# The routing's keys behind the low part of the last outputs in a fused attention and expert kernel

## Chip, cores and metric

One core of one Trainium2 chip. The metric is the device time of one launch in microseconds (us), as the median of the runs.

## What is computed

A gated cross-attention layer and a mixture-of-experts layer on 32 batches of 256 tokens of width 256:

```
x = x + tanh(g_xattn) * LN_affine(softmax(q k^T / 8) v Wout)   # q from LN(x), 16 heads of 64,
                                                               # k, v from 77 context rows and one null row
h = LN(x)
w = top-8 of sigmoid(h Wr + br), divided by their sum          # 32 experts
x = x + tanh(g_ffn) * (shared(h) + sum_e w[t, e] * expert_e(h))
expert_e(h) = (silu(h Wg + bg) * (h Wu + bu)) Wd + bd          # width 128
```

Products in f32 are made as three products of a high part (rounded to fp32r) and a low part (the difference): `split_product` (L142). ScalarE makes the high part while it copies a bank out of PSUM, VectorE the low part by a subtraction.

## The kernel before

**Phases.** A context phase makes all keys and values and stores them in DRAM. Then the attention loop runs over steps b = -2 .. 33, and the expert phase over 16 dense rounds (the shared expert on all tokens) and 159 pages of 512 token rows, each page of one expert.

**A step of the attention loop.** Step b does the attention of batch b, the output projection, layer norms and x1 of batch b - 1, and the routing of batch b - 2. Each engine has a written order of work; semaphores alone tie the engines together.

- *TensorE* (`tensor`, `step` at L1401): `similarity(0)` and `similarity(1)`, the scores of half the heads for each of the two token tiles, and then the names of `RING` (L93) in order, each of which writes one of four PSUM banks: X (transpose of the next but one batch's normed x), N2 (transpose of the rows to be routed), Oa and Ob (output projection of the batch before, line L144 to L146 with `wo`), T0a .. T3b (transposes of probabilities), L (router logits), R (mask sums that give each row its place), Q0 .. Q3 (queries of the next batch), PV0a .. PV1b (outputs, transposed). Behind Oa stand `similarity(2)` and `similarity(3)`. `similarity(u)` waits until the exponentials of u - 2 are done, since it overwrites their scores (L1295). Oa waits until PV1b's low part of the step before is made (L1370). `free` (L1308) makes each name wait until its bank was evicted: T3a for PV0a's low part, R for `centre`, which reads Ob.
- *ScalarE* (`scalar`): the exponentials `exp` (L935), 32 a step, each with its sum, then the high parts (L947).
- *VectorE* (`vector`, `step` at L1218): `maximum(u)` (L1037) of scores, `normalise(u)` (L1043 to L1052), the low parts in the order of `EVICTED` (`low`, L1184), and between these, where `ROUTE_AFTER` (L109) says so, the stages of the routing (`route`, L1088). Layer norm: `statistics` (L1058, L1062), `centre` (z, L1070), `residual` (x1, L1078). The next batch's `maximum(0)` stands behind PV1a.
- *GpSimd* (`gpsimd`, `step` at L863): 16 indirect scatters a step (L854), which put the 256 rows of a batch eight times into pages; `weigh` (L861); x1's bias (L885); and `make_rstd` (L841 to L848), `make_rstd(1)` for the output norm, on which `centre` waits, and `make_rstd(2)` for the norm of x1.
- *SyncE* issues all plain DMAs.

**The routing's last stages.** `key` (L1142 to L1147) makes three results: key = (slot + 1) * mask, a new page_end, and top_key, the eight largest keys of a token. `kept` (L1151) turns top_key into kept_index, the row numbers that the scatters of the next step use. `match` (L1191) and `sum_weights` (L1201) read key and top_key in the next step. Line numbers are the same in both kernels.

`ROUTE_AFTER` names, for a low part, the stages that VectorE does right behind it. The keys were done behind PV1a, so after `maximum(0)` of the next batch and before PV1b's low part:

Of the kernel before, what the change touches and what calls it, by code (L numbers as in the profile page):

```python
# [106 lines left out]
AHEAD_FILLS, AHEAD_PAGES = 3, 3  # L107

ROUTE_AFTER = {"T1a": ["logits", "top", "mask"], "PV0b": ["placed"], "Q3": ["opened", "page", "moved", "slot"],  # L109
               "PV1a": ["key"], "PV1b": ["kept"]}  # L110

ROUTE = ["biased", "logits", "top", "without_top", "mask", "placed", "opened", "over", "page", "moved", "owner", "page_shift",
         "over_shift", "cursor", "grown", "slot", "key", "page_end", "top_key", "kept"]
# [1961 lines left out]
```

How the kernel before makes its waits and increments, by code:

```python
            def load_x(batch):  # L262
                if batch >= 3:
                    sp.wait_ge(tile_measured, batch - 1)
                sp.dma_start(x_rows[x_slot(batch)][:, :, 0:D], x_tiles[batch]).then_inc(tile_loaded[x_slot(batch)], 16)
# [1 line left out]
            def load_piece(i):  # L267
                if i >= STAGES:
                    sp.wait_ge(w_lo, i - STAGES + 1)
                sp.dma_start(staged(i), pieces[i][0]).then_inc(w_loaded[i % STAGES], 16)
# [19 lines left out]
            def step(g):  # L290
                for name in CRING:
                    if not made_in(name, g):
                        continue
                    if name[0] == "K" and int(name[2]) % KPART == KPART - 1:
                        i, unit = int(name[1]), key_unit(name, g)
                        first = int(name[2]) // KPART * KPART * M
                        sp.wait_ge(hi, at(CRING, name, g))
                        sp.dma_start(keys_out[:, g * CG + i * CBATCHES:g * CG + (i + 1) * CBATCHES, first:first + KPART * M],
                                     keys[unit % KSLOTS][:, :, :, :].rearrange("p b q m -> p b (q m)")).then_inc(keys_stored[unit % KSLOTS], 16)
                    if name[0:2] == "K1":
# [3 lines left out]
                    elif name[0] == "V" and name[2] == "1":  # L304
                        unit = value_unit(name, g)
                        sp.wait_ge(lo, at(CRING, name, g))
                        t = int(name[1])
# [108 lines left out]
            def moments(batch):  # L416
                dve.wait_ge(tile_measured, batch + 1)
                for t in range(TT):
```

## Time and profile before

| | us |
|---|---|
| median of 3 runs | 2119.76 |
| lowest, highest | 2118.06, 2122.13 |
| profiled execution | 2123.7 |
| its span in the profile | 2122.0 |
| TensorE busy | 1996.5 |
| VectorE busy | 1667.2 |
| ScalarE busy | 1384.1 |
| GpSimd busy | 1205.9 |

The granted TensorE clock is 0.977 on the mean. The profile is of one execution; DVE is VectorE, ACT ScalarE, POOL GpSimd, PE TensorE's matmuls and PEld its weight loads. An idle time in brackets stands before the instruction of its row, with what ended it. Times in a timeline are from the start of the span.

### The profile page before, as it was taken

The numbers are of one execution on the slowest core, as the hardware profiler recorded it, in microseconds if no ns is written. First come the engines' busy times: TensorE is split into PE (matmuls) and PEld (weight loads), VectorE is DVE, ScalarE is ACT, GpSimd is POOL, SyncE is SP. The second block draws the span as 40 slices with busy tenths as digits, with TensorE's granted clock in tenths as the row PEclk, the third lists the DMA queues.
The fourth block names the chain that finished last, engine by engine and source line by source line (L and its number), as shares of the span: only waits on it lengthen the run. The fifth ranks groups of instructions, "written<-read, shape, count | busy, mean of one in ns | idle before, by whom it ended". The sixth has DMA issues, their size and how long they took to land. (4 is left out here: it accounts for less than half of the span.)

```text
span 2122.0 us, 42583 instructions
## 1 busy us (share of the span) xinstructions
PE 1996.5 (94%) x13762; PEld 1832.7 (86%) x13762; DVE 1667.2 (79%) x3996; ACT 1384.1 (65%) x4030; POOL 1205.9 (57%) x1323
## 2 busy tenths in 40 slices
PE   7999689999999999999997899999999999999995
PEld 7888589999999999999986788989888888888884
DVE  4433158888888888888886766768999999999996
ACT  3322267777777777777773267777877777777771
POOL 0000203777777777777777500017777777777775
PEclk9999899999999999999997899999999999999997
DMA  9664678977777777777786999999999999999998
GB/s 279 211 192 169 243 219 268 293 241 242 241 243 245 244 246 244 246 244 235 246 266 221 330 336 287 286 293 385 404 401 398 396 393 389 395 395 393 392 362 281
DMA packets 401109, 625.61 MB, mean 295 GB/s; under 512 B 171000, under 2 KB 275161, under 8 KB 398425
## 3 DMA queue, kind: packets, MB, share of 16 engines
q1 hardware_dynamic: 351736, 488.60, 68.1%
q0 software_dynamic: 49152, 134.28, 17.6%
q8 instruction: 112, 1.84, 0.4%
q14 instruction: 109, 0.88, 0.1%
HBM read 315.08 MB, written 307.63 MB: 293 GB/s over the span
## 5 line engine op out<-in xcount | busy, mean ns | idle before, releaser
L1714 POOL DMA_INDIRECT parts<-results_dram,kept_index x512 | 517.7, 1011 | 382.6 <-DMA results_dram<-y 218.8
L854 POOL DMA_INDIRECT pages_dram<-rows,kept_index x512 | 509.9, 996 | 158.5 <-issue 139.2
L935 ACT ACTIVATE exps<-sim,minus_max 128x78 f32<-128x78 f32 x1024 | 321.0, 366 | 35.9 <-DVE minus_max L1037 35.7
L935 ACT ACTIVATION_READ_ACCUMULATOR exps<-sim,minus_max 128x1 f32 x1024 | 253.1, 248 | 0.0
L1735 ACT ACTIVATE w_h<-w_raw 128x768 fp32r<-128x768 f32 x159 | 134.0, 843 | 155.7 <-DMA w_raw<-in_experts 155.7
L1823 DVE SCALAR_TENSOR_TENSOR parts<-parts,kept_weight 128x256 f32<-128x256 f32 x448 | 213.6, 477 | 2.6 <-DMA parts<-dense_dram 1.4
L1920 PE MATMUL xps<-ident,xin 128*128 128x128 f32 x1272 | 167.2, 275 | 20.1 <-DVE wq_l L1785 9.8
L1797 DVE TENSOR_TENSOR w_l<-w_raw,w_h 128x768 fp32r<-128x768 f32 x159 | 151.7, 954 | 40.3 <-ACT w_h L1735 40.1
L144 PE MATMUL yps<-w_h,hid_h 128*128 128x256 f32 x636 | 179.5, 282 | 0.3
L146 PE MATMUL yps<-w_l,hid_h 128*128 128x256 f32 x636 | 178.8, 281 | 0.0
L145 PE MATMUL yps<-w_h,hid_l 128*128 128x256 f32 x636 | 178.5, 281 | 0.0
L1742 ACT ACTIVATE y<-yps 128x512 f32<-128x512 f32 x318 | 171.7, 597 | 1.5 <-PE yps L146 1.5
L1920 PEld LDWEIGHTS xps<-ident,xin 128*128 128x128 f32 x1272 | 140.8, 141 | 29.0 <-issue 24.1
L1299 PE MATMUL sim<-kT,qT 128*128 128x156 f32 x1024 | 155.5, 303 | 7.2 <-issue 3.8
L144 PE MATMUL ring<-xnT_h,wq_h 128*128 128x256 f32 x512 | 156.4, 305 | 3.7 <-DVE outT_l L1184 1.8
L1785 DVE TENSOR_TENSOR wq_l<-xps,wq_h 128x512 fp32r<-128x512 f32 x212 | 143.0, 686 | 18.5 <-ACT wq_h L1729 18.5
L1766 ACT ACTIVATE hid_h<-up_ps 128x512 fp32r<-128x512 f32 x175 | 103.3, 591 | 81.3 <-DVE up_ps L1874 80.1
L1299 PEld LDWEIGHTS sim<-kT,qT 128*128 128x128 f32 x1024 | 142.8, 194 | 12.4 <-issue 10.5
L144 PE MATMUL ring<-wo_h,outT_h 128*128 128x256 f32 x512 | 148.7, 290 | 3.4 <-DVE outT_l L1184 0.5
L1874 DVE SCALAR_TENSOR_TENSOR up_ps<-up_ps,w_raw,act_gate 128x512 f32<-128x512 f32 x159 | 120.1, 755 | 37.7 <-PE up_ps L146 36.2
L146 PE MATMUL ring<-xnT_l,wq_h 128*128 128x256 f32 x512 | 144.7, 283 | 0.0
L1037 DVE TENSOR_REDUCE minus_max<-sim 128x8 f32<-128x624 f32 x128 | 102.2, 799 | 54.0 <-PE sim L1299 54.0
(261 smaller groups left out, 6638.7 us busy)
## 6 DMA issues: line engine op xcount, KB each, us to landing
xin<-pages_dram SPq DMA_DIRECT2D x159, 512.0 KB, 10.7
results_dram<-y SPq DMA_DIRECT2D x159, 512.0 KB, 9.7
w_raw<-in_experts SPq DMA_DIRECT2D x159, 385.0 KB
pages_dram<-blank SPq DMA_DIRECT2D x108, 512.0 KB, 3.9
pages_dram<-blank SPq DMA_DIRECT2D x20, 1024.0 KB, 6.2
values_dram<-values SPq DMA_DIRECT2D x16, 1024.0 KB
v_main<-values_dram SPq DMA_DIRECT2D x64, 256.0 KB
keys_dram<-keys SPq DMA_DIRECT2D x16, 616.0 KB, 4.3
```

Of the source, the lines that this page charges most:

```text
L144: eng.matmul(out, left[0], right[0], start=start, stop=False)
L145: eng.matmul(out, left[1], right[0], start=False, stop=False)
L146: return eng.matmul(out, left[0], right[1], start=False, stop=stop)
L854: pool.indirect_dma_start(dram["pages"], bass.IndirectOffsetOnAxis(ap=kept_index[:, at:at + 1].bitcast(U32), axis=0), buffer(batch)[:, k / ...
L935: last = act.activation(exps[u % 2][:, h, :], scores(u)[:, h // 4, h % 4, :], ACT.Exp, bias=minus_max[u][:, h:h + 1], accum_out=row_sum[u] ...
L1299: last = pe.matmul(sim[u % 2][:, i // 2, (i % 2) * 2 * J:(i % 2 + 1) * 2 * J], qT[:, pair, tt * P:(tt + 1) * P], kT[:, pair, :], start=Tru ...
L1714: pool.indirect_dma_start(parts[slot(batch, t)][:, k, :], None, done, bass.IndirectOffsetOnAxis(ap=kept_index[:, at:at + 1].bitcast(U32), ...
L1742: last = act.activation(y[s][:, q:q + 2, :], yps[:, q:q + 2, :], ACT.Copy)
L1785: dve.tensor_tensor(xT[m % XT][1][:, c, :], xps[:, c, :], xT[m % XT][0][:, c, :].bitcast(F32), ALU.subtract).then_inc(x_lo, 1)
L1797: dve.tensor_tensor(w_split[s][1][:, :], w_raw[s][:, 0:EW], w_split[s][0][:, :].bitcast(F32), ALU.subtract).then_inc(w_lo, 1)
L1823: dve.scalar_tensor_tensor(out=out, in0=part[:, k, :], scalar=kept.weight[:, at:at + 1], in1=part[:, TOPK, :], op0=ALU.mult, op1=ALU.add). ...
L1920: last = pe.transpose(xps[:, c, q * P:(q + 1) * P], xin[s][:, q, c * P:(c + 1) * P], ident[:, :])
```

## The change

The stage `key` moves from behind PV1a to behind PV1b, in front of `kept`. Everything that the stages compute is as before.

```diff
-               "PV1a": ["key"], "PV1b": ["kept"]}
+               "PV1b": ["key", "kept"]}
```

Only VectorE's order differs. The first place is the end of a step in the middle of the loop (steps 2 to 30): outT_l is the low part of PV1a and then of PV1b, minus_max<-sim the next batch's first maximum and then its second. Before:

```order
L1139 TENSOR_TENSOR slot<-placed_to,over_shift 128x64
L1184 TENSOR_TENSOR outT_l<-ring,outT_h 128x512
L1037 TENSOR_REDUCE minus_max<-sim 128x8
L1142 SCALAR_TENSOR_TENSOR key<-slot,mask 128x64
L1144 TENSOR_TENSOR page_end<-page_end,grown 128x32
L1147 MAX top_key<-key 128x8 x2
L1184 TENSOR_TENSOR outT_l<-ring,outT_h 128x512
L1151 TENSOR_SCALAR kept_index<-top_key 128x16
L1037 TENSOR_REDUCE minus_max<-sim 128x8
```

And changed:

```order
L1139 TENSOR_TENSOR slot<-placed_to,over_shift 128x64
L1184 TENSOR_TENSOR outT_l<-ring,outT_h 128x512
L1037 TENSOR_REDUCE minus_max<-sim 128x8
L1184 TENSOR_TENSOR outT_l<-ring,outT_h 128x512
L1142 SCALAR_TENSOR_TENSOR key<-slot,mask 128x64
L1144 TENSOR_TENSOR page_end<-page_end,grown 128x32
L1147 MAX top_key<-key 128x8 x2
L1151 TENSOR_SCALAR kept_index<-top_key 128x16
L1037 TENSOR_REDUCE minus_max<-sim 128x8
```

PV1b's low part has moved up over four instructions (top_key is two), and kept_index now follows top_key directly.

The second place is step 31, the last with outputs, on VectorE again; there is no next batch, so no maximum stands there, and kept_weight is the first instruction of step 32. Changed:

```order
L1139 TENSOR_TENSOR slot<-placed_to,over_shift 128x64
L1184 TENSOR_TENSOR outT_l<-ring,outT_h 128x512 x2
L1142 SCALAR_TENSOR_TENSOR key<-slot,mask 128x64
L1144 TENSOR_TENSOR page_end<-page_end,grown 128x32
L1147 MAX top_key<-key 128x8 x2
L1151 TENSOR_SCALAR kept_index<-top_key 128x16
L1201 TENSOR_REDUCE kept_weight<-of_key 128x16
```

Both low parts stand in front of the whole routing group. In steps 32 and 33, which have no outputs, nothing moves. So the move happens in 30 steps.

## Rows read from the trace of the kernel before

**Rows 1.** The page, span and busy time (engine, us, share, instructions).
```profile
span 2122.0 us, 42583 instructions
...
PE 1996.5 (94%) x13762; PEld 1832.7 (86%) x13762; DVE 1667.2 (79%) x3996; ACT 1384.1 (65%) x4030; POOL 1205.9 (57%) x1323
```

**Rows 2.** Timeline of POOL (start, us, engine, line, operation, count, [idle before <-releaser]).
```profile
611.59 0.19 POOL L841 TENSOR_TENSOR var_eps<-mean_var,eps_col 128x2 f32<-128x2 f32 x1 [1.27 <-DVE mean_var L1062]
...
618.54 1.07 POOL L854 DMA_INDIRECT pages_dram<-rows,kept_index  x1 [0.30 <-issue]
...
622.43 0.96 POOL L854 DMA_INDIRECT pages_dram<-rows,kept_index  x1 [0.31 <-DVE weight L1175]
...
624.68 1.30 POOL L861 TENSOR_TENSOR of_key<-of_key,weight 128x512 f32<-128x512 f32 x1
...
631.41 0.72 POOL L843 TENSOR_TENSOR rstd<-var_eps,minus_half 128x2 f32<-128x2 f32 x1
```

**Rows 3.** Timeline of DVE, statistics in step 12 and centring in step 13.
```profile
610.13 0.42 DVE L1184 TENSOR_TENSOR pT_l<-ring,pT_h 112x256 fp32r<-112x256 f32 x1 [0.59 <-ACT pT_h L947]
610.48 0.74 DVE L1058 BATCH_NORM_STATS2 stats<-x 128x6 f32<-128x256 f32 x2
611.26 0.25 DVE L1062 BATCH_NORM_AGGREGATE mean_var<-stats 128x2 f32<-128x6 f32 x2
...
632.16 0.87 DVE L1070 SCALAR_TENSOR_TENSOR z<-ring,mean_var,scale_row 128x256 f32<-128x256 f32 x2 [0.69 <-POOL rstd L843]
```

**Rows 4.** Timeline of DVE, centring in steps 2, 3, 4 and 31.
```profile
336.53 0.87 DVE L1070 SCALAR_TENSOR_TENSOR z<-ring,mean_var,scale_row 128x256 f32<-128x256 f32 x2
...
363.09 0.87 DVE L1070 SCALAR_TENSOR_TENSOR z<-ring,mean_var,scale_row 128x256 f32<-128x256 f32 x2
...
390.46 0.88 DVE L1070 SCALAR_TENSOR_TENSOR z<-ring,mean_var,scale_row 128x256 f32<-128x256 f32 x2 [0.69 <-POOL rstd L843]
...
1116.13 0.88 DVE L1070 SCALAR_TENSOR_TENSOR z<-ring,mean_var,scale_row 128x256 f32<-128x256 f32 x2 [0.69 <-POOL rstd L843]
```

**Rows 5.** Timeline of DVE around the keys, and the step's last maximum.
```profile
614.75 0.81 DVE L1037 TENSOR_REDUCE minus_max<-sim 128x8 f32<-128x624 f32 x1 [1.07 <-PE sim L1299]
615.47 0.21 DVE L1142 SCALAR_TENSOR_TENSOR key<-slot,mask 128x64 f32<-128x64 f32 x1
...
615.72 0.29 DVE L1147 MAX8 top_key<-key 128x8 f32<-128x32 f32 x2
615.92 0.68 DVE L1184 TENSOR_TENSOR outT_l<-ring,outT_h 128x512 fp32r<-128x512 f32 x1
616.51 0.17 DVE L1151 TENSOR_SCALAR kept_index<-top_key 128x16 int32<-128x16 f32 x1
...
623.26 0.80 DVE L1037 TENSOR_REDUCE minus_max<-sim 128x8 f32<-128x624 f32 x1
```

**Rows 6.** Timeline of PE's weight loads and of ACT's exponentials.
```profile
616.71 0.19 PEld L144 LDWEIGHTS ring<-wo_h,outT_h 128*128 128x128 f32 x1 [0.31 <-DVE outT_l L1184]
...
620.72 0.56 PEld L1299 LDWEIGHTS sim<-kT,qT 128*128 128x128 f32 x4 [0.17 <-issue]
...
615.59 0.33 ACT L935 ACTIVATE exps<-sim,minus_max 128x78 f32<-128x78 f32 x1 [0.33 <-DVE minus_max L1037]
...
620.31 0.29 ACT L935 ACTIVATION_READ_ACCUMULATOR exps<-sim,minus_max 128x1 f32 x1
```

**Rows 7.** Waits of PE's weight loads, 400 to 900 us (us in total, times, longest).
```profile
PEld ring L1348 <- DVE outT_l L1184: 7.7, 18, 0.4
PEld ring L1390 <- DVE z L1070: 4.7, 18, 0.3
```

**Rows 8.** Timeline of DVE at the end of attention.
```profile
1127.77 0.69 DVE L1184 TENSOR_TENSOR outT_l<-ring,outT_h 128x512 fp32r<-128x512 f32 x1 [0.34 <-ACT outT_h L947]
1128.38 0.17 DVE L1151 TENSOR_SCALAR kept_index<-top_key 128x16 int32<-128x16 f32 x1
...
1136.70 0.41 DVE L1215 TENSOR_TENSOR shared_row_l<-shared_row,shared_row_h 1x256 fp32r<-1x256 f32 x1
```

## The prediction

> **What bounds the kernel.** I read the page first, then the timelines of one step of the attention loop, engine by engine, then the waits. TensorE is busy for 94% of the span and GpSimd for 57% [rows 1]. These shares are a mean over the context phase, the attention loop (about 290 to 1128 us) and the expert phase. The change touches only the loop, so the loop must be read by itself.
>
> In its timeline GpSimd is never free but once a step. It waits 1.27 us for the variance of x1, works on var_eps at 611.59, and then has twelve scatters, two table operations and the next statistics behind one another until rstd ends at 632.13 [rows 2]. VectorE has stood 0.69 us for exactly that rstd when it starts z at 632.16 [rows 3]. From z the path goes on: z frees the bank, PV0a's low part follows and releases T3a, T3b comes behind Q2, ScalarE copies it, VectorE's pT_l waits 0.59 us for ScalarE, then the statistics of x1 run, and GpSimd gets them at the next var_eps [rows 3]. That is a **closed loop**: 632.16 - 611.59 = 20.6 us in GpSimd's queue and some 6.3 us through the other three engines. None of its members is an instruction that moves. The wait of 0.69 us stands before z in step 4 and still in step 31; the 27 steps between take 1116.13 - 390.46 = 725.67 us, **26.88 us a step**. Between steps 2 and 3, where z does not wait, a step took 363.09 - 336.53 = **26.56 us** [rows 4]. So TensorE, VectorE and ScalarE could turn in 26.56 and are held to 26.88 by GpSimd: a margin of 0.32 us a step.
>
> **The change, part by part.** Nothing is added or removed. In 30 steps (2 to 31) PV1b's low part moves ahead of key, page_end and top_key.
>
> (a) *The low part is earlier.* It starts at 615.92, behind a group that began at 615.47 [rows 5]. Its input is ready, so it starts at 615.47: 0.45 us earlier, and ends at 616.15.
>
> (b) *TensorE's first output projection.* Its first weight load waited 0.31 us and came 616.71 - 616.60 = 0.11 us behind the low part [rows 5, 6]. Now the condition is met at 616.26, and the load could have run from 616.71 - 0.31 = 616.40. So 0.31 us of waiting goes, in each step.
>
> (c) *Where these 0.31 us go.* The fourth group of scores needs the second group of exponentials. ScalarE's exponentials run without a gap from 615.59 to 620.31 + 0.29 = 620.60, started by the maximum that ends at 614.75 + 0.81 = 615.56 [rows 5, 6]. That maximum stands in front of everything that moves. TensorE's weight load for the fourth group comes at 620.72 after 0.17 us idle [rows 6], 0.12 us behind the last exponential, as in (b). TensorE arrives there 0.31 us earlier and waits 0.48 us in place of 0.17. The gain is spent four microseconds after it is made: net **0**. And were it not, TensorE stands again at the mask matmuls (4.7 us in 18 steps, 0.26 each) and at T3a (7.7 in 18, 0.43 each) [rows 7], both held by z and what follows, that is by GpSimd.
>
> (d) *kept_index loses its cover.* It reads top_key, and the low part stood between them. Behind an independent instruction the next starts 0.09 us before the end (low part 615.92 + 0.68 = 616.60, kept_index 616.51) [rows 5]; behind the one it depends on it starts 0.04 after it (statistics 610.48 + 0.74 = 611.22, aggregation 611.26) [rows 3]. So kept_index and all of VectorE behind it come **0.13 us later** each step. The cover: 0.69 us before z [rows 3], GpSimd's multiplication at 624.68, which wants the last maximum, over at 624.06 and now at 624.19 [rows 2, 5], and the scatter at 618.54, which wants kept_index, over at 616.68 and now at 616.81 [rows 2, 5]. If VectorE's delay passes to TensorE through a bank it is 0.13 against the 0.26 at the mask matmuls [rows 7]. In steps 3 to 30 the loop's 26.88 stays: 28 x 0 = **0**. If the cover were gone it would be 28 x 0.13 = 3.6 us.
>
> The Trainium skill speaks against (d): its page VectorE: DVE Perf Modes, section The DRAIN you can't avoid, says that the semaphore between chained operations costs nothing extra. By that rule (d) would be 0 and nothing would need a cover; the rows above show 0.13.
>
> (e) *The first block, step 2*, lies before GpSimd's loop closes: 0 to 0.13 us. I take 0, since the loop closes later, on a wait of GpSimd.
>
> (f) *The last block, step 31.* Here VectorE waits 0.34 us for ScalarE and starts the last low part at 1127.77 [rows 8]; the key group was done in the shade of that wait. Now it stands behind: kept_index starts at 1127.77 + 0.69 - 0.09 + 0.45 + 0.13 = 1128.95 in place of 1128.38 [rows 8], **0.57 us later**. From there to the shared weights' low part, which ends at 1136.70 + 0.41 = 1137.11 [rows 8], VectorE is a chain of work that TensorE's first expert matmul waits for. Ends: 0, if a later wait swallows it, and 0.57; I take 0.57, because that chain has no slack I can see.
>
> Sum: 0 + 0 + 0.57 = **+0.6 us** on a profiled execution of 2123.7 us (span 2122.0 and 1.7 around it), so 2124.3. That execution lies 3.9 us above the median of the runs, 2119.76, within what single runs differ by. On the median: **2120.3 us**.
>
> **The rivals.**
>
> *Faster: TensorE is the bound.* For it: 94% busy, and a wait of 0.31 us that certainly goes. Against it: the 0.17 before the fourth scores and 0.69 before z. If both were softer than they look, 29 steps x 0.31 = 9.0 us would be won: 2119.8 - 9.0 + 0.6 = **2111.4**. Chance 0.10.
>
> *Slower: VectorE's queue becomes the bound.* From the maximum at 614.75 to the next z VectorE has no wait, so its delay is passed on whole. It decides as soon as a step gets 0.32 us longer [rows 4]. If the moved group and kept_index lose 0.5 us together (the group's 0.45 and a part of (d)), each step costs 0.5 - 0.32 = 0.18, 28 x 0.18 = 5.0, and 0.6 at the end: **2125.4**. For it: the margin is small. Against: only 0.13 can be found. Chance 0.07.
>
> *Slower: scatters grow.* Another overlap of VectorE and GpSimd could lengthen a scatter, which is in the closed loop whole. The rows have one of 1.07 us and one of 0.96 [rows 2]. Two longer ones a step would be 28 x 0.22 = 6.2: 2119.8 + 6.2 + 0.6 = **2126.6**. Chance 0.04, since the moved instructions shift by half a microsecond only. The Trainium skill's page SBUF — State Buffer, section SBUF: two separate sides, gives a mechanism for it: an exclusive lock of the port pair that VectorE and GpSimd share. The trace does not show it here: the scatter at 622.43 took the short 0.96 us [rows 2].
>
> *The change does nothing at all* can be ruled out as a failure of the edit: the order shows the move in every step. As a time it is the forecast.
>
> **How the numbers follow.** My forecast of no measurable change has 0.79. Three runs differ by 4 us, so 0.2% (4.2 us, 2115.5 to 2124.0) is about what can be told from nothing. Faster by more: 0.10. Slower by more: 0.07 + 0.04 = 0.11. The range takes the forecast with its ends (0 to 28 x 0.13 + 0.57 = 4.2 above 2119.8, so up to 2124.0) and below it room for a part of (b) that gets through, 0.13 of 0.31 in 29 steps, 3.8: 2116.0 to 2124.0.
>
> **What would show it.** In the changed kernel's profile: the low part directly behind the maximum and kept_index 0.04 behind top_key; the 0.31 us before the output projection gone and some 0.48 before the fourth scores; z still waiting for rstd, for about 0.56; GpSimd's wait for the variance still 1.27, and the step still 26.88. I am wrong if the step is shorter than 26.8 or the wait before z is gone; then the loop through GpSimd was not what held the kernel.

## The result: slower by 0.26%, a delay that its cover did not cover

The changed kernel takes **2125.63 us**, the median of 9 runs (2122.79 to 2130.47), against 2120.07 for the kernel before in as many runs (2117.23 to 2124.27): a ratio of **1.0026, 95% interval 1.0017 to 1.0034**, so 3.6 to 7.2 us slower. The forecast was 2120.3 and no measurable change, its range ended at 2124.0, and it gave slower a chance of 0.11. It was wrong. Here and below a ratio is worked out from the single runs without the slow ones (one of the kernel before took 2461 us at a granted clock of 0.75), so it is not the quotient of the medians.

The page of the changed kernel, its span and busy times (engine, us, share, instructions):

```profile
span 2124.0 us, 42583 instructions
...
PE 1990.0 (94%) x13762; PEld 1827.1 (86%) x13762; DVE 1670.7 (79%) x3996; ACT 1383.5 (65%) x4030; POOL 1206.1 (57%) x1323
```

As before [rows 1], this tells nothing: the shares are the same. The timeline of VectorE in the changed kernel, around the keys of step 12, and centring in steps 4, 13 and 31:

```profile
389.74 0.88 DVE L1070 SCALAR_TENSOR_TENSOR z<-ring,mean_var,scale_row 128x256 f32<-128x256 f32 x2 [0.70 <-POOL rstd L843]
...
615.08 0.81 DVE L1037 TENSOR_REDUCE minus_max<-sim 128x8 f32<-128x624 f32 x1 [1.08 <-PE sim L1299]
615.80 0.68 DVE L1184 TENSOR_TENSOR outT_l<-ring,outT_h 128x512 fp32r<-128x512 f32 x1
616.40 0.22 DVE L1142 SCALAR_TENSOR_TENSOR key<-slot,mask 128x64 f32<-128x64 f32 x1
...
616.65 0.29 DVE L1147 MAX8 top_key<-key 128x8 f32<-128x32 f32 x2
616.97 0.31 DVE L1151 TENSOR_SCALAR kept_index<-top_key 128x16 int32<-128x16 f32 x1
617.05 0.80 DVE L1037 TENSOR_REDUCE minus_max<-sim 128x8 f32<-128x624 f32 x1
...
618.55 0.69 DVE L1191 TENSOR_TENSOR of_key<-key,top_key 128x512 f32<-128x512 f32 x1
...
632.65 0.88 DVE L1070 SCALAR_TENSOR_TENSOR z<-ring,mean_var,scale_row 128x256 f32<-128x256 f32 x2 [0.70 <-POOL rstd L843]
...
1118.82 0.88 DVE L1070 SCALAR_TENSOR_TENSOR z<-ring,mean_var,scale_row 128x256 f32<-128x256 f32 x2 [0.70 <-POOL rstd L843]
```

The low part stands directly behind the maximum, 0.72 after its start, as the keys did before [rows 5]. The second maximum comes 617.05 - 615.08 = 1.97 us behind the first; before it was 616.59 - 614.75 = 1.84 us [rows 5], the second start being this row of VectorE's timeline in the kernel before:

```profile
616.59 0.80 DVE L1037 TENSOR_REDUCE minus_max<-sim 128x8 f32<-128x624 f32 x1
```

That is the delay of VectorE: **0.13 us**. And z still waits 0.70 for rstd, as before [rows 3]; had the wait swallowed the delay, 0.56 would be left. Yet the 27 steps from 389.74 to 1118.82 take 729.08 us, **27.00 us a step against 26.88** [rows 4].

The timeline of GpSimd in the changed kernel, the same step (start, us, operation, [idle before <-releaser]):

```profile
611.92 0.19 POOL L841 TENSOR_TENSOR var_eps<-mean_var,eps_col 128x2 f32<-128x2 f32 x1 [1.27 <-DVE mean_var L1062]
...
618.88 1.20 POOL L854 DMA_INDIRECT pages_dram<-rows,kept_index  x1 [0.30 <-issue]
620.38 0.96 POOL L854 DMA_INDIRECT pages_dram<-rows,kept_index  x1 [0.30 <-issue]
...
622.91 0.96 POOL L854 DMA_INDIRECT pages_dram<-rows,kept_index  x1 [0.30 <-DVE weight L1175]
...
630.41 1.16 POOL L854 DMA_INDIRECT pages_dram<-rows,kept_index  x1 [0.30 <-issue]
```

GpSimd still waits 1.27 for the variance, so the closed loop through GpSimd still sets the step, and a member of it has grown. It is the first scatter of GpSimd's step: **1.20 us in place of 1.07** [rows 2]. Most scatters take 0.96. What stands beside it is VectorE's comparison of_key (L1191, 128x512, both inputs in SBUF). The same row in the kernel before, from VectorE's timeline, with the probabilities (L1051, of the same kind) beside the fourth scatter of the step, at 622.43:

```profile
618.09 0.69 DVE L1191 TENSOR_TENSOR of_key<-key,top_key 128x512 f32<-128x512 f32 x1
...
622.45 0.70 DVE L1051 TENSOR_TENSOR probs<-exps,row_inv 128x512 f32<-128x512 f32 x1
```

Before, the comparison ends at 618.09 + 0.69 = 618.78 and the scatter at 618.54 + 1.07 = 619.61 [rows 2], 0.83 later. Changed, it ends at 618.55 + 0.69 = 619.24 and the scatter at 618.88 + 1.20 = 620.08, 0.84 later. The scatter began while the comparison ran, at the same time after var_eps in both (6.95 and 6.96 us), and its end follows the comparison's end. So the comparison's delay goes into the scatter whole, and from there into rstd, z and the next step.

The sum: 28 steps x 0.126 = 3.5 us, and 0.6 at the end of attention (below), **4.1 us, 0.19%**, within the measured 0.17 to 0.34%. The medians lie 5.6 us apart; the 1.5 us between the two are within the noise, and no run shows whether anything is behind them.

### The profile page after: what moved, and what is told of

The parts are those of the page before. It is cut to its first block, busy times and chain, and to the rows that moved or that the text cites. A ratio compares the mean times of both kernels' runs of the same rounds, so it can differ in the third digit from the quotient of the medians.

```text
span 2124.0 us, 42583 instructions
## 1 busy us (share of the span) xinstructions
PE 1990.0 (94%) x13762; PEld 1827.1 (86%) x13762; DVE 1670.7 (79%) x3996; ACT 1383.5 (65%) x4030; POOL 1206.1 (57%) x1323
## 3 DMA queue, kind: packets, MB, share of 16 engines
q8 instruction: 112, 1.84, 0.4%
## 4 chain that ended last, share of the span: by engine, by line
PE 29%; DVE 22%; DMA 15%; POOL 10%; issue 8%; ACT 3%; SPq 2%; DVEq 0%; POOLq 0%; ACTq 0%
DMA w_raw<-in_experts 13%; POOL pages_dram L854 6%; PE ring L144 4%; DVE parts L1823 4%; PE ring L146 4%; PE ring L145 4%; PE sim L1299 2%; DVE minus_max L1037 2%; PE xps L1920 2%; DVE outT_l L1184 2%; POOL of_key L861 2%; DVE hid_l L1880 2%; POOL x L885 2%; DVE up_ps L1874 2%; DVE wq_l L1785 2%
## 5 line engine op out<-in xcount | busy, mean ns | idle before, releaser
L145 PE MATMUL ring<-xnT_h,wq_l 128*128 128x256 f32 x512 | 144.4, 282 | 0.0
```

What stands on the lines that cost most here:

```text
L145: eng.matmul(out, left[1], right[0], start=False, stop=False)
```

## Experiments

Every run stands against runs of the kernel before on the same chip in the same session. Steps are means of 27 steps between waits of z. Two theories stood at first. *The lock*: a scatter that begins while VectorE works on two SBUF inputs ends 0.84 us after that work (a name for what the rows show, not a mechanism seen in them), and of_key is where the 0.13 us gets into the loop. Its rival: something else of the move costs it, the younger kept_index, the group of keys at its new time, or VectorE's queue as such.

### e1: the kept stage behind the next maximum

The low part and the keys stay where the change puts them; kept_index alone moves behind the second maximum, where it depends on nothing just made.

```diff
             if here:
                 maximum(1, b)
+            if 3 <= b <= B - 1:
+                route("kept", b - 1, 1 - par, h)
...
-                        route(part, b, par, h)
+                        if part != "kept" or b > B - 2:
+                            route(part, b, par, h)
```

> Changed kernel, with kept_index moved on behind the next batch's second maximum, so that it no longer stands directly behind top_key. Lock theory (the first scatter of a step cannot get on while VectorE's two-input multiplication-like comparison of_key runs, and ends 0.83 us after it): of_key comes 0.12 us earlier again against the loop, the first scatter falls from 1.20 back to 1.07 us, the step from 27.00 to 26.88, the time to the kernel before's, 2120 within 0.1%. Rival, the young index (the scatter is long because kept_index, which it reads, was made shortly before): kept_index is now 0.7 us later, the scatter is 1.20 or longer, the step at least 27.00. Rival, the key group (its two-input operations stand beside a scatter now): they stay where they are, step 27.00.

Measured: 2120.63 us against 2120.92, ratio 1.0001 [0.9992, 1.0011]; step 26.87. Its timelines, VectorE and GpSimd:

```profile
614.55 0.16 DVE L1151 TENSOR_SCALAR kept_index<-top_key 128x16 int32<-128x16 f32 x1
...
615.40 0.69 DVE L1191 TENSOR_TENSOR of_key<-key,top_key 128x512 f32<-128x512 f32 x1
```

```profile
615.87 1.06 POOL L854 DMA_INDIRECT pages_dram<-rows,kept_index  x1 [0.30 <-issue]
```

The comparison ends at 616.09, the scatter at 616.93: 0.84. With the delay gone the scatter is 1.06 and the loss is gone, though the keys are still made behind the low part and kept_index is made still later. That leaves neither the moved group nor the age of kept_index as a cause.

### e2: the kernel before, with VectorE delayed at that place

Nothing is moved. Two small operations on a spare tile stand behind kept_index, which compute nothing that is used.

```diff
+    spare = sb("spare", [P, 4, TT * TOPK])
...
+                if b <= B - 2:
+                    for i in range(2):
+                        dve.tensor_scalar(spare[:, i, :], ones[:, 0:TT * TOPK], -1.0, None, ALU.add)
```

> Kernel before, its order untouched, with two small operations more on VectorE behind kept_index (each subtracts one from 16 columns of a constant, into tiles that nobody reads), some 0.08 to 0.12 us each, 0.2 together. Lock theory: of_key is 0.2 us later, the first scatter 1.07 + 0.2 = 1.27, the step 26.88 + 0.2 = 27.08, the time 2120 + 28 x 0.2 = 2125.6, though z still waits about 0.7 us for rstd. Cover theory of my prediction (a delay of VectorE is swallowed by the wait before z): step 26.88, 2120. Young index: kept_index is not later, 2120.

Measured: 2124.88 against 2120.92, ratio 1.0014 [1.0005, 1.0023]; step 27.02. Timelines of VectorE and of GpSimd, and VectorE's waits from 400 to 900 us (us in total, times, longest):

```profile
614.14 0.38 DVE L1156 TENSOR_SCALAR spare<-ones 128x16 f32<-128x16 f32 x2
...
615.80 0.69 DVE L1195 TENSOR_TENSOR of_key<-key,top_key 128x512 f32<-128x512 f32 x1
```

```profile
616.11 1.22 POOL L855 DMA_INDIRECT pages_dram<-rows,kept_index  x1 [0.30 <-issue]
```

```profile
DVE z L1071 <- POOL rstd L844: 13.2, 19, 0.7
```

The two operations cost 0.15 us and not the 0.2 expected, since each starts 0.07 behind the one before it. The scatter grows by 0.15, the step by 0.15, and z waits its 0.7 as ever: VectorE loses time in front of a wait that is as long afterwards. 28 x 0.146 = 4.1 us is 0.19%, in the interval. So the delay alone, with no instruction moved, makes the step longer.

### e3: the changed kernel, with the comparison out of the scatter's way

The comparison gets a second buffer for its output and runs in front of the weights' sum of the batch before, 0.8 us earlier.

```diff
-            if batch:
-                dve.wait_ge(kept.summed, batch)
-            dve.tensor_tensor(of_key[:, :, :, :], ...
+            if batch > 1:
+                dve.wait_ge(kept.summed, batch - 1)
+            dve.tensor_tensor(of_key[batch % 2][:, :, :, :], ...
...
+            if b >= 3:
+                match(b - 3)
             if b >= 4:
                 sum_weights(b - 4)
-            if b >= 3:
-                match(b - 3)
```

> Changed kernel, with a second buffer for of_key so that the comparison that makes it can stand before the sum of the batch before and not behind it: of_key 0.78 us earlier. Lock theory: it ends before the first scatter of the step begins, which then takes 0.96 us; the step falls from 27.00 to 27.00 - 0.24 = 26.76, the time from 2125.6 by 28 x 0.24 = 6.7 to 2119. Young index: nothing of that changes, 2125.6.

Measured: 2121.82 against 2120.92, ratio 0.9997 [0.9985, 1.0009]; most steps 26.83, where the changed kernel has 27.00 (with one of 27.85 the mean is 26.87).

```profile
617.21 0.68 DVE L1191 TENSOR_TENSOR of_key<-key,top_key 128x512 f32<-128x512 f32 x1
617.81 0.68 DVE L1201 TENSOR_REDUCE kept_weight<-of_key 128x16 f32<-128x512 f32 x1
```

```profile
618.31 0.96 POOL L854 DMA_INDIRECT pages_dram<-rows,kept_index  x1 [0.30 <-issue]
...
629.61 1.23 POOL L854 DMA_INDIRECT pages_dram<-rows,kept_index  x1 [0.30 <-issue]
```

The first scatter is 0.96, the short one. It still begins while VectorE works on 512 elements a partition, until 618.49, but on one SBUF input: that does not hold it. (Held, it would have ended at 618.49 + 0.84 = 619.33 and taken 1.02, so this row alone is a narrow test; the counts in the last section are a wide one.) Of the 0.24 us won there 0.07 is lost again in the scatter before rstd, 1.23 for 1.16, which at the new phase meets the probabilities earlier in their work.

### e4: the same for the kernel before, a miss

> Kernel before with the same second buffer and the comparison early. Lock theory: first scatter 0.96 in place of 1.07, the step 26.88 - 0.11 = 26.77, the time 2120 - 28 x 0.11 = 2117, that is the same step as the changed kernel with the comparison early; what is left between these two is the last block, 0.57 us. Young index: 26.88, 2120.

Measured: **2126.35** against 2120.92, ratio 1.0025 [1.0015, 1.0036]; step 27.09. The edit that was to be worth 3 us costs 5. Timelines of VectorE and GpSimd, and VectorE's waits from 400 to 900 us:

```profile
620.54 0.69 DVE L1051 TENSOR_TENSOR probs<-exps,row_inv 128x512 f32<-128x512 f32 x1
```

```profile
619.34 0.96 POOL L854 DMA_INDIRECT pages_dram<-rows,kept_index  x1 [0.30 <-issue]
620.60 1.47 POOL L854 DMA_INDIRECT pages_dram<-rows,kept_index  x1 [0.30 <-DVE weight L1175]
...
628.62 0.99 POOL L854 DMA_INDIRECT pages_dram<-rows,kept_index  x1 [0.30 <-issue]
```

```profile
DVE z L1070 <- POOL rstd L843: 16.4, 18, 1.0
```

The first scatter lost its 0.11 as expected (the three in front of 620.60, the first of which begins at 616.81, take 0.96). But then the fourth begins at 620.60, 0.06 after the probabilities, and takes 1.47: it ends at 622.07, again 0.84 behind the end of VectorE's work at 621.23. In the kernel before the same scatter began 0.02 *before* the probabilities and took 0.96 [rows 2]. Eight hundredths of a microsecond decide half a microsecond. The balance is 0.51 - 0.11, less the 0.16 that the scatter before rstd now saves (0.99 for 1.15), = +0.24 a step; measured +0.21. The mechanism holds, and my forecast of one scatter's gain forgot the others.

### e12 and e18: relief of the loop

If the loop through GpSimd sets the step, one scatter less in it must shorten the step until another loop bounds. `make_rstd(1)` moves up by one scatter, in the kernel before (e12) and in the changed one (e18):

```diff
-                scatter(b, range(5, 8))
+                scatter(b, range(5, 7))
...
-                scatter(b, range(8, 12))
+                scatter(b, range(7, 12))
```

> The kernel before with make_rstd(1) one scatter earlier, a third time, for a chip on which the kernel before takes its usual 2120. Loop theory (z waits for GpSimd's queue, and that sets the step): step 26.65, 2114. Rival, TensorE alone bounds the loop: 26.88, 2120. Rival, VectorE's queue is no looser than GpSimd's, or another scatter is hit by the lock at the new phase: 26.88 or more.

> The changed kernel with make_rstd(1) one scatter earlier, for an undisturbed chip. Lock theory with a free scatter: the step and the time of before plus relief (26.63, 2112.6). Rival, VectorE's queue bounds: step 26.75, 3.4 us above it. Rival, TensorE bounds and wins its 0.31: step down to 26.3.

Measured: e12 **2112.63** against 2119.19, ratio 0.9972 [0.9961, 0.9983], step 26.63; e18 2116.79 against 2121.56, ratio 0.9980 [0.9971, 0.9990], step 26.75. The kernel before with this relief beats both kernels. GpSimd and VectorE in e12:

```profile
606.45 0.19 POOL L841 TENSOR_TENSOR var_eps<-mean_var,eps_col 128x2 f32<-128x2 f32 x1 [0.55 <-DVE mean_var L1062]
```

```profile
626.27 0.87 DVE L1070 SCALAR_TENSOR_TENSOR z<-ring,mean_var,scale_row 128x256 f32<-128x256 f32 x2
```

And in e18, with the waits of TensorE's weight loads from 400 to 900 us last:

```profile
617.72 1.21 POOL L854 DMA_INDIRECT pages_dram<-rows,kept_index  x1 [0.30 <-issue]
```

```profile
617.40 0.69 DVE L1191 TENSOR_TENSOR of_key<-key,top_key 128x512 f32<-128x512 f32 x1
...
630.72 0.87 DVE L1070 SCALAR_TENSOR_TENSOR z<-ring,mean_var,scale_row 128x256 f32<-128x256 f32 x2
```

```profile
PEld ring L144 <- DVE outT_l L1184: 11.4, 18, 0.6
PEld sim L1299 <- issue: 9.8, 19, 0.5
```

In both z stands without a wait: the loop through GpSimd no longer bounds. The first line of e18's waits is not the one before the output projection; it is 0.63 us each before the queries' product, where TensorE stands for a low part that VectorE makes behind z. Of the lock alone one would have expected e18 to be as fast as e12, since rstd is early enough for a scatter of 1.21. It is 0.12 us a step slower, by its timelines. What is left is VectorE's own queue, from the first maximum to z, which has no wait in it now and passes the 0.13 on: from 400 to 1080 us that stretch takes 16.67 us in e12 and 16.80 in e18 on the mean, and the way back from z to the next first maximum 9.96 and 9.95. So the delay costs the same in either regime, by two different ways: through the scatter where GpSimd bounds, directly where VectorE does. And TensorE's 0.31 us are won in neither: in e18 too it stands 0.5 before the fourth scores, 9.8 us in 19 times. The two ratios differ by 0.08%, less than their intervals are wide; the 0.12 is read from the traces.

The relief gave less than a scatter, and the lock shows there too. rstd now ends 19.54 us after the first var_eps of the step in place of 20.54, one microsecond earlier, though a scatter of 1.15 with 0.30 of issue is gone. GpSimd and then VectorE in e12:

```profile
603.47 1.16 POOL L854 DMA_INDIRECT pages_dram<-rows,kept_index  x1 [0.30 <-issue]
...
624.54 0.65 POOL L841 TENSOR_TENSOR var_eps<-mean_var,eps_col 128x2 f32<-128x2 f32 x1
```

```profile
602.93 0.87 DVE L1078 SCALAR_TENSOR_TENSOR x<-z,rstd,x 128x256 f32<-128x256 f32 x2
...
624.46 0.69 DVE L1051 TENSOR_TENSOR probs<-exps,row_inv 128x512 f32<-128x512 f32 x1
```

The tiny var_eps takes 0.65 us in place of 0.21, since it begins under the probabilities and ends 0.04 after them. And a scatter that was short is held by x1's sum (z and x, both in SBUF), whose second half ends at 603.80: the scatter ends 0.83 later.

### Twelve runs on slower chips

Twelve more runs fell on chips on which the kernel before itself took 2700 to 2750 us, with steps of mostly 33 to 38 us and a mean granted clock of about 0.88. Up to 7 us of a step are waits before the scores and the maxima whose releaser the trace does not name (in e5 70.0 us before the maxima from 400 to 900 us). They say nothing of a loop of 26.9 us. Among them were the reliefs of e12 and e18 (`make_rstd` one scatter earlier), the changed kernel again, and the changed kernel with e1's and e18's edits together ("both cures"; e7, e10, e14 and e17 are this one kernel). The medians are of all runs:

| run | us | kernel before | ratio |
|---|---|---|---|
| e5, relief of the kernel before | 2781.61 | 2739.38 | 1.0208 [1.0126, 1.0289] |
| e8, the same | 2725.27 | 2702.63 | 1.0215 [1.0133, 1.0297] |
| e6, relief of the changed kernel | 2755.72 | 2739.38 | 1.0162 [1.0087, 1.0236] |
| e9, the same | 2696.49 | 2702.63 | 1.0109 [1.0006, 1.0211] |
| e13, the same | 2766.04 | 2751.28 | none |
| e16, the same | 2719.59 | 2705.47 | 1.0044 [0.9979, 1.0108] |
| e7, both cures | 2766.57 | 2739.38 | none |
| e10, both cures | 2750.83 | 2702.63 | 1.0199 [1.0048, 1.0350] |
| e14, the same | 2769.95 | 2751.28 | none |
| e17, the same | 2750.59 | 2705.47 | none |
| e11, the changed kernel | 2692.11 | 2702.63 | 1.0127 [1.0024, 1.0230] |
| e15, the same | 2759.24 | 2751.28 | none |

> Kernel before, with make_rstd(1) on GpSimd one scatter earlier in each step (two scatters in front of it and five behind, in place of three and four). Loop theory (z waits for GpSimd's queue, and that sets the step): rstd is ready 1.26 us earlier, the 0.69 us before z go, the step falls from 26.88 towards the 26.56 of the steps in which z does not wait, say 26.65, and the time by 28 x 0.23 = 6 to 2114. Rival, TensorE alone bounds the loop: its waits only move, step 26.88, 2120.

> The change under the same relief of GpSimd. Lock theory: what the move costs, it costs through the first scatter; with GpSimd no longer in the closed loop a longer scatter is free, and the kernel stands with the one before plus relief, step 26.65, 2114. Rival, VectorE's queue is then the bound: its 0.12 us stay, step 0.12 above the one before plus relief, 3.4 us in all. Rival, TensorE is then the bound and the 0.31 us before the output projection are won: step up to 0.3 below, 8 us in all.

> Both cures: the low part early, kept_index behind the second maximum, make_rstd(1) one scatter earlier. If VectorE's queue is the bound once GpSimd is relieved, this has the same length of that queue as the kernel before and TensorE's wait gone: the step of before plus relief, 26.65, or less by up to 0.3 if TensorE decides. Time 2106 to 2114, the best of all.

> The kernel before with make_rstd(1) one scatter earlier, once more, on a chip on which the kernel before takes its usual 2120. Loop theory: step 26.65, 2114. Rival, TensorE alone bounds the loop: 26.88, 2120.

> The changed kernel with the same relief, once more. Lock theory: the longer scatter is free now, the same as before plus relief. Rival, VectorE's queue bounds: step 0.12 above it, 3.4 us in all. Rival, TensorE bounds and wins its 0.31: step up to 0.3 below it.

> Low part early, kept_index behind the second maximum, make_rstd(1) one scatter earlier, once more. Step as before plus relief or up to 0.3 less; time 2106 to 2114.

> The changed kernel itself beside the others on the same chip. Lock theory: first scatter 1.20, step 27.00, 28 x 0.126 = 3.5 and the last block's 0.6, so 4.1 us or 0.19% above the kernel before. If the 5.6 us of the first comparison hold, something outside the loop costs 1.5 more.

> The changed kernel with make_rstd(1) one scatter earlier, on a chip on which the kernel before takes its usual 2120. Lock theory with a free scatter: the same as before plus relief (e12, 2112.6). Rival, VectorE's queue bounds: step 0.12 above e12's, 3.4 us in all, 2116. Rival, TensorE bounds and wins its 0.31: step up to 0.3 below e12's.

> Low part early, kept_index behind the second maximum, make_rstd(1) one scatter earlier. If VectorE's queue bounds after the relief: the step of e12. If TensorE does: up to 0.3 less, down to 2104.

> The changed kernel itself beside the others on the same chip. Lock theory: first scatter 1.20, step 27.00, 28 x 0.126 = 3.5 and the last block's 0.6, so 4.1 us or 0.19% above the kernel before. If the 5.6 us of the first comparison hold, something outside the loop costs 1.5 more.

> The changed kernel with make_rstd(1) one scatter earlier, again for an undisturbed chip. Lock theory with a free scatter: the step and the time of before plus relief (26.63, 2112.6). Rival, VectorE's queue bounds: step 26.75, 3.4 us above it. Rival, TensorE bounds and wins its 0.31: step down to 26.3.

> Low part early, kept_index behind the second maximum, make_rstd(1) one scatter earlier. If VectorE's queue bounds after the relief: step 26.63, 2112.6. If TensorE does: down to 26.3, 2104.

No gain or loss of the relief follows from the table. Most ratios stand above 1, but by the medians e9 and e11 are 0.2 and 0.4% below the kernel before, so not even the sign is sure. What limits the kernel there was not followed.

## Why the prediction was wrong, point by point

**The loop through GpSimd, 26.88 us, and its margin of 0.32: right.** z waits in every step for rstd and GpSimd for the variance, in both kernels; relieving it gave 26.63 (e12), where 26.56 had been read from steps 2 and 3, so the margin was 0.25.

**(a) and (b), the low part earlier and TensorE's 0.31 us: right.** Waits of the weight loads from 400 to 900 us (us in total, times, longest), before the output projection and the queries in the kernel before:

```profile
PEld ring L144 <- DVE outT_l L1184: 9.2, 37, 0.3
```

And in the changed kernel:

```profile
PEld ring L144 <- DVE outT_l L1184: 3.2, 18, 0.2
PEld sim L1299 <- issue: 9.8, 19, 0.5
PEld ring L1348 <- DVE outT_l L1184: 7.7, 18, 0.4
PEld ring L1390 <- DVE z L1070: 4.6, 18, 0.3
```

The 6.0 us that went are the 0.31 of each step; the 3.2 left stand before the queries.

**(c) The gain comes back as a wait before the fourth scores: right**, 9.8 / 19 = 0.52 each where 0.48 was forecast, and the waits at T3a and at the mask matmuls are as they were [rows 7].

**(d) is the step that failed.** Its first half held: kept_index follows top_key by its end, and VectorE is 0.13 later. The second half said that 0.69 us before z cover this, and that the multiplication and the scatter need their inputs later than they come, so 28 x 0 = 0. All of that is true of the *semaphores*: every wait named there is as long as before. But the comparison of_key and the scatter beside it are tied by no semaphore, and through them the delay went around the cover: **28 x 0.126 = 3.5 us in place of 0**. With it the sum is 2119.8 + 4.1 = 2123.9, still 1.7 under the median measured, which no term here accounts for. I had named 28 x 0.13 = 3.6 as the price "if the cover were gone", and taken it as the far end of the range. My signs of being wrong, a step under 26.8 or no wait before z, did not come; what came was a wait of 0.70 where 0.56 was forecast, with a step of 27.00.

**(e)** 0 to 0.13, taken as 0: right as far as the traces tell. From z in step 2 to z in step 3 it is 362.19 - 335.63 = 26.56 us in the changed kernel too.

**(f) The last block: right in size.** VectorE's timeline in the changed kernel, step 31 and behind it:

```profile
1128.24 0.69 DVE L1184 TENSOR_TENSOR outT_l<-ring,outT_h 128x512 fp32r<-128x512 f32 x1 [0.59 <-ACT outT_h L947]
...
1129.45 0.32 DVE L1151 TENSOR_SCALAR kept_index<-top_key 128x16 int32<-128x16 f32 x1
...
1137.79 0.41 DVE L1215 TENSOR_TENSOR shared_row_l<-shared_row,shared_row_h 1x256 fp32r<-1x256 f32 x1
```

kept_index follows the last low part by 1.21 us; before by 0.61 [rows 8]. From the low part to shared_row_l it is 9.55 us, before 8.93 [rows 8]: 0.60 to 0.62 longer, where 0.57 was forecast. That the launch pays it in full no run tells; it is 0.03% of the time.

**The rivals.** "Scatters grow" was the right one, with a chance of 0.04, and its 2126.6 is near the 2125.63 measured by luck, for a size that is not the one found: not two scatters by 0.22, but one by 0.13. I dismissed it because the scatter at 622.43 took the short 0.96 us with VectorE's probabilities at work beside it. That row proves nothing: it began at 622.43 and the probabilities at 622.45, so it was there first. With it falls my sentence that the trace does not show the lock; the row of 1.07 us showed it. The two rows to look at were the scatter at 618.54 and the comparison at 618.09, and only the first was among my rows. The other slower rival, VectorE's queue, is not what bounds the changed kernel, but it is what bounds e18.

The Trainium skill's page SBUF — State Buffer, section SBUF: two separate sides, says that VectorE and GpSimd share ports under an exclusive lock, by which the one that comes first holds them for its instruction; of VectorE's operations outside its two-port modes it names those with two SBUF inputs, against a GpSimd operation that reads SBUF. For a scatter that begins during a two-input operation the traces agree: it ends 0.82 to 0.85 us after that operation, in eight kernels. Had I gone by that rule of the Trainium skill at the row where it bears, with VectorE's 0.13, the sum would have been 28 x 0.13 + 0.57 = 4.2 us and the forecast 2124.0, an estimate.

**Why the profiled spans differ by 2.0 us only.** Windows of the two traces from z in step 31 to the last low part, before and then changed (stretch: us, busy us of PE, PEld, DVE, ACT, POOL, then PEclk, DMA share, GB/s):

```profile
1116.10:1127.80 11.70, 8.89 (x52) 8.21 (x50) 8.21 (x30) 3.94 (x8) 7.15 (x10) 0.73 0.35 125
```

```profile
1118.80:1128.20 9.40, 6.51 (x52) 5.84 (x50) 7.68 (x25) 3.78 (x8) 5.99 (x9) 0.96 0.39 142
```

The same 52 matmuls ran at a mean granted clock of 0.73 in the profiled execution of the kernel before and at 0.96 in that of the changed one. From z at 1116.13 to the last low part at 1127.77 it is 11.64 us, from 1118.82 to 1128.24 only 9.42: 2.2 us less, more than half of what the loop costs. In the kernel before the clock stood at 0.5, which is 1.2 GHz, from about 1112 to 1119 and again from 1123 to 1126 us, after TensorE had been idle for most of 1110 to 1114; in the changed kernel from 1116 to 1119, after it had been idle for most of 1113 to 1116. This does not go with the change: the same stretch takes 11.68 and 12.42 us at 0.73 and 0.72 in e3 and e18, which have the changed order, and 9.41 at 0.95 in e1, which has it too; in the old order it is 11.73 at 0.72 in e2 and 10.17 at 0.92 in e12.

So one pair of spans is no measure of the change. Their 2.0 us are -0.7 up to z in step 4 (390.46 and 389.74), +3.4 in the 27 steps, -2.2 here, +0.6 in the last block and +0.9 behind it.

## What to carry to other kernels

A wait covers a delay only if the delayed engine touches the bounding loop nowhere else: look beside every GpSimd instruction in the loop for a VectorE operation on two SBUF inputs that is under way when the instruction begins, and treat the end of that operation as if it were a semaphore. An operation with an input in PSUM, or with one input, held no scatter here. To judge such a pair, read which of the two began first; a hit moves by as much as VectorE does, and a miss by 0.02 us says nothing for a kernel in which one of them shifts by 0.1. Where GpSimd closes the loop, one scatter out of it was worth 0.28% (e12).

## What the runs showed of the hardware

**A scatter waits for VectorE's operations on two SBUF inputs, whole.** Where an operation had begun and the scatter begins inside it:

| kernel | VectorE's operation ends | scatter ends | difference |
|---|---|---|---|
| before, of_key | 618.78 | 619.61 | 0.83 |
| before, probs | 630.26 | 631.10 | 0.84 |
| changed, of_key | 619.24 | 620.08 | 0.84 |
| changed, probs | 630.74 | 631.57 | 0.83 |
| e1, of_key | 616.09 | 616.93 | 0.84 |
| e2, of_key | 616.49 | 617.33 | 0.84 |
| e4, probs | 621.23 | 622.07 | 0.84 |
| e12, x | 603.80 | 604.63 | 0.83 |
| e18, of_key | 618.09 | 618.93 | 0.84 |

From 400 to 1080 us the kernel before has 25 scatters of over 1.09 us and the changed one 50, since of_key's now pass that bound too; all 75 began during such an operation. The growth is real time of GpSimd and not a matter of how spans are recorded: from the start of the first scatter to the next it is 620.38 - 618.88 = 1.50 us in the changed kernel, and 1.26 between two short ones. Alone a scatter takes 0.96, so one that is held ends as if it had 0.84 left when the operation ends: it grows only if more than 0.12 us of the operation are left when it begins.

**It is the second input in SBUF that matters.** The eight traces of e1 to e4, e12, e18 and the two kernels, from 400 to 1080 us, have 1182 scatters that directly follow another scatter, begin at least 0.03 us into an operation of VectorE, and would take more than 1.02 us if it held them:

| VectorE's operation | scatters | us, shortest to longest |
|---|---|---|
| two inputs, both in SBUF (of_key, probs, x) | 351 | 1.04 to 1.47 |
| two inputs, one in PSUM (low parts, placed_to) | 481 | 0.96 to 0.97 |
| one input, in PSUM (minus_max) | 313 | 0.96 |
| one input, in SBUF (kept_weight, affinity) | 37 | 0.96 to 0.97 |

All of the first kind are held, and none of the others. In the kernel before alone it is 50 of 50 and 0 of 110, so its trace could have told it before any experiment.

**The other way round it holds VectorE hardly at all.** The probabilities that begin 0.02 us after a scatter take 0.70 us for 0.69, and none of 22 scatters in the kernel before that began up to 0.15 us ahead of such an operation is longer than 0.96; the operations took 0.69 to 0.72. The turn lies just behind a common start: scatters that began up to 0.02 us after the operation were not held, those from 0.05 us on were, at 1.43 to 1.47. By the rule of the Trainium skill's page SBUF — State Buffer, section SBUF: two separate sides, the later comer would be stopped for the whole instruction; here VectorE lost 0.03 us at most, so for a scatter of 0.96 us the measurement decides.

**What stays open.** Why a scatter holds VectorE so little was not tested. Both cures together never ran on a chip with steps of 26.9 us. And what holds the steps to 33 to 38 us on the slower chips was not looked into.
